# A gated recurrence plus a ternary-weight matmul on eight cores: start-up work reordered, transposed tiles copied out by VectorE

## What is computed

```python
xn = layernorm(x)                                  # x: [8, 4096, 2048] f32
a  = tanh(xn @ Wa.T + ba);  b = tanh(xn @ Wb.T + bb)   # Wa, Wb: [64, 2048]
h_t = a_t * h_(t-1) + b_t                          # scan over the 4096 rows
scale = mean(|weight|)                             # weight: [2048, 2048]
w_t = clip(round(weight / scale), -1, 1)           # -1, 0 or 1
out = x + (xn + h @ Wout.T + bout) + (xn @ (w_t * scale).T + bias)
```

## Time and profile before

| what | value |
| --- | --- |
| median of three runs | 747.67 us |
| the profiled execution | 748.4 us |
| its span on the slowest core (core 6) | 746.9 us |
| spans of the eight cores | 742.0 to 746.9 us |
| mean granted TensorE clock of core 6 | 0.992 |
| PE busy, share of the span | 586.5 us, 79% |
| DVE busy, share of the span | 348.9 us, 47% |
| ACT busy, share of the span | 235.4 us, 32% |

### The profile page before, as it was taken

How to read it: one execution, slowest core, us unless ns; L and a number is a source line. 1 busy time by engine, 2 the same in 40 slices (tenths; PEclk the granted TensorE clock), 3 DMA queues, 4 the chain that set the end, 5 groups by cost and what they waited for, 6 DMA issues and landing times.

```text
span 746.9 us, 11239 instructions; the slowest of 8 cores (742.0 to 746.9 us)
## 1 busy us (share of the span) xinstructions
PE 586.5 (79%) x3740; PEld 310.9 (42%) x3804; DVE 348.9 (47%) x303; ACT 235.4 (32%) x250; POOL 217.9 (29%) x742
## 2 busy tenths in 40 slices
PE   0112202447899999999999999999999999999995
PEld 0111202434444444444454444444444445444442
DVE  0000316985555444555544555544555544555521
ACT  0665302562522323222223332233222222322220
POOL 0000061225043333333333334333333333433400
PEclk9999999999899999999999999999999999999998
DMA  7996008873123343332333333333333233222321
GB/s 234 340 330 196 0 0 278 267 251 106 57 113 117 128 146 141 142 121 114 114 113 113 114 113 114 121 137 139 149 134 113 114 113 114 114 113 113 114 91 79
DMA packets 16831, 103.02 MB, mean 138 GB/s; under 512 B 4326, under 2 KB 4358, under 8 KB 4358
## 3 DMA queue, kind: packets, MB, share of 16 engines
q1 hardware_dynamic: 9350, 51.96, 21.2%
q0 software_dynamic: 7424, 50.34, 17.7%
HBM read 68.73 MB, written 33.55 MB: 137 GB/s over the span
## 4 chain that ended last, share of the span: by engine, by line
PE 65%; DMA 11%; ACT 8%; issue 4%; ACTq 4%; DVEq 3%; DVE 2%; POOLq 2%; SPq 1%; POOL 0%
PE pffn L560 16%; PE pffn L546 15%; PE pffn L556 14%; PE pffn L543 13%; DMA vv<-wf 7%; ACT xnT L302 4%; ACTq L301 3%; PE pab L534 3%; DMA outb<-wf 2%; PE ptr L570 2%; DVE wbn L368 2%; ACT xnT L298 1%; DVEq L367 1%; DMA sqscr<-wf 1%; DVEq L362 1%
## 5 line engine op out<-in xcount | busy, mean ns | idle before, releaser
L560 PE MATMUL pffn<-w_rhs,xnT 128*128 128x512 bf16 x512 | 195.1, 381 | 3.3 <-ACT w_rhs L259 1.7
L546 PE MATMUL pffn<-w_rhs,xnT 128*128 128x512 bf16 x496 | 188.0, 379 | 1.6
L556 PE MATMUL pffn<-w_rhs,xnT 128*128 128x512 bf16 x480 | 182.9, 381 | 0.0
L543 PE MATMUL pffn<-w_rhs,xnT 128*128 128x512 bf16 x465 | 176.2, 379 | 0.0
L346 DVE TENSOR_REDUCE sums<-sx 128x1 f32<-128x2048 f32 x32 | 73.1, 2286 | 140.4 <-DMA sx<-x 140.1
L298 ACT COPY xnT<-ptr 128x1024 bf16<-128x1024 bf16 x31 | 31.4, 1012 | 240.1 <-PE ptr L570 240.1
L605 POOL TENSOR_SCALAR mm_<-sums 128x1 f32<-128x1 f32 x32 | 7.4, 232 | 333.8 <-DVE sqscr L348 310.9
L280 ACT ACTIVATE xnb<-sx,nmr,yr 128x2048 bf16<-128x2048 f32 x31 | 64.9, 2093 | 99.5 <-POOLq L639 99.5
L397 DVE SCALAR_TENSOR_TENSOR outb<-pffn,negs,vv 128x1024 f32<-128x1024 f32 x32 | 41.1, 1284 | 117.7 <-PE pffn L586 102.4
L480 PE MATMUL ptr<-sidn,wbn 128*128 128x128 bf16 x256 | 28.3, 296 | 62.5 <-DVE wbn L368 60.2
L556 PEld LDWEIGHTS pffn<-w_rhs,xnT 128*128 128x128 bf16 x512 | 50.3, 98 | 62.5 <-issue 2.9
(11 more groups left out here) (109 smaller groups left out, 587.4 us busy)
## 6 DMA issues: line engine op xcount, KB each, us to landing
sx<-x SPq DMA_DIRECT2D x32, 1024.0 KB, 5.3
y<-outb POOLq DMA_DIRECT2D x32, 1024.0 KB, 5.7
outb<-wf POOLq DMA_DIRECT2D x11, 1024.0 KB, 6.6
wtile<-wf SPq DMA_DIRECT2D x8, 1024.0 KB, 10.9
vv<-wf SPq DMA_DIRECT2D x8, 1024.0 KB, 10.9
sqscr<-wf POOLq DMA_DIRECT2D x5, 1024.0 KB, 6.4
wasb<-wa SPq DMA_DIRECT2D x1, 512.0 KB
wosb<-wout SPq DMA_DIRECT2D x1, 512.0 KB, 11.3
```

Of the source, the lines that this page charges most:

```text
L543: tensor.matmul(pffn[:, 0:512], lhs, w_rhs[:, 2048 * c:2048 * c + 512], start=st_, stop=False)
L546: tensor.matmul(pffn[:, 512:1024], lhs, w_rhs[:, 2048 * c + 512:2048 * c + 1024], start=st_, stop=False)
L556: tensor.matmul(pffn[:, 1024:1536], lhs, w_rhs[:, 2048 * c + 1024:2048 * c + 1536], start=st_, stop=False)
L560: ins = tensor.matmul(pffn[:, 1536:2048], lhs, w_rhs[:, 2048 * c + 1536:2048 * c + 2048], start=st_, stop=False)
```

## The change

The change has two parts.

In the start-up, SP loads `Wout` in 16 pieces at once after the small inputs, then the two x tiles, then `Wb` (after the first cast), and only then the first-pass weight tiles. ACT and PE do `Wa`, `Wb` and `Wout` before the first pass instead of behind it. POOL issues the loads of the second pass first of all, the first three without any wait, and runs `chain` for x tiles 0 and 1 only after all sixteen and the 16 small transfers to `wocv`. DVE computes the sums of x tiles 0 and 1 after the sixteenth ternary tile. PE and ACT do the first x tile after all of the weight. The second half of the columns of tile 0 now follows its first half directly.

In the loop, the two copies from `ptr` to `xnT` go from ACT to DVE, where they stand between the sums of tile k+2 and the two `pffn` instructions.

```diff
 sync:
+            for j in range(NW):
+                sync.dma_start(out=wosb[:, 64 * j:64 * (j + 1)],
+                               in_=wo_d[128 * j:128 * (j + 1), :]
+                               ).then_inc(s_wol, 16)
             sync.dma_start(out=sx[:, 0:D], in_=x_d[0:TT, :]).then_inc(s_x0, 16)
             sync.dma_start(out=sx[:, D:2 * D],
                            in_=x_d[TT:2 * TT, :]).then_inc(s_x1, 16)
+            sync.wait_ge(s_cast, 1)
+            sync.dma_start(out=wasb[:, :], in_=wb_d[:, :]).then_inc(s_wbl, 16)
             for j in range(NW):
...
-            sync.dma_start(
-                out=wosb[:, :].rearrange("p (j s) -> p j s", j=NW),
-                in_=wo_d[:, :].rearrange("(j p) s -> p j s", p=128)
-            ).then_inc(s_wol, 16)
-            sync.wait_ge(s_cast, 1)
-            sync.dma_start(out=wasb[:, :], in_=wb_d[:, :]).then_inc(s_wbl, 16)
 scalar, in the loop:
-                if k < NT - 1:
-                    j = k + 1
-                    jsl = j % 2
-                    scalar.wait_ge(s_tr, 2 * k + 3)
-                    if k >= 1:
-                        scalar.wait_ge(s_ffn, k)
-                    scalar.drain()
-                    scalar.copy(xnT[:, jsl * D:jsl * D + 1024],
-                                ptr[:, 0:1024]).then_inc(s_xnT, 1)
-                    scalar.wait_ge(s_tr, 2 * k + 4)
-                    scalar.drain()
-                    scalar.copy(xnT[:, jsl * D + 1024:jsl * D + 2048],
-                                ptr[:, 1024:2048]).then_inc(s_xnT, 1)
 vector, in the loop:
                 if k < NT - 2:
                     sums_sqs(k + 2)
+                if k < NT - 1:
+                    j = k + 1
+                    jsl = j % 2
+                    vector.wait_ge(s_tr, 2 * k + 3)
+                    if k >= 1:
+                        vector.wait_ge(s_ffn, k)
+                    vector.drain()
+                    vector.tensor_copy(xnT[:, jsl * D:jsl * D + 1024],
+                                       ptr[:, 0:1024]).then_inc(s_xnT, 1)
+                    vector.wait_ge(s_tr, 2 * k + 4)
+                    vector.drain()
+                    vector.tensor_copy(xnT[:, jsl * D + 1024:jsl * D + 2048],
+                                       ptr[:, 1024:2048]).then_inc(s_xnT, 1)
                 vector.wait_ge(s_mix, 2 * k + 1)
 gpsimd:
+            for j in range(NW):
+                if j >= 3:
+                    g.wait_ge(s_tern, j - 2)
...
             chain(0)
             chain(1)
-            for j in range(NW):
-                if j < 3:
-                    g.wait_ge(s_wabs, 10 + 2 * j)
-                    if j == 2:
-                        g.wait_ge(s_sums, 2)
-                else:
-                    g.wait_ge(s_tern, j - 2)
```

More of the change, by code:

```diff
@@ L240, in _ @@
             for j in range(NW):
-                if j == 11:
-                    scalar.wait_ge(s_stats, 1)
-                    scalar.drain()
[L244 to L251, removed]
-                    scalar.wait_ge(s_tr, 2)
-                    scalar.drain()
-                    scalar.copy(xnT[:, 1024:2048], ptr[:, 1024:2048]
-                                ).then_inc(s_xnT, 1)
                 for grp in range(2):
@@ L420, in _ @@
         def _(tensor):
-            tensor.wait_ge(s_ms, 1)
-            for j in range(NW):
-                tensor.wait_ge(s_wabs, j + 1)
-                for c in range(NCH):
-                    ins = tensor.matmul(
-                        spare[:, 0:1],
-                        xnT[:, (j % 2) * D + 128 * c:(j % 2) * D + 128 * (c + 1)],
-                        onescolb[:, :],
-                        start=(j == 0 and c == 0),
-                        stop=(j == NW - 1 and c == NCH - 1))
-                ins.then_inc(s_pam, 1)
             tensor.wait_ge(s_cast, 1)
@@ L452, in _ @@
             ins.then_inc(s_wotr, 1)
+            tensor.wait_ge(s_cvecv, 1)
+            for j in range(NW):
+                tensor.wait_ge(s_wabs, j + 1)
+                for c in range(NCH):
+                    ins = tensor.matmul(
+                        spare[:, 0:1],
+                        xnT[:, (j % 2) * D + 128 * c:(j % 2) * D + 128 * (c + 1)],
+                        onescolb[:, :],
+                        start=(j == 0 and c == 0),
+                        stop=(j == NW - 1 and c == NCH - 1))
+                ins.then_inc(s_pam, 1)
             tensor.wait_ge(s_acc, 16)
@@ L466, in _ @@
                           start=True, stop=True).then_inc(s_bc, 5)
-            def wtr(j):
+            for j in range(NW):
                 sl = j % 2
@@ L484, in wtr @@
                     ins.then_inc(s_wtr, 1)
-            for j in range(13):
-                wtr(j)
-            tensor.wait_ge(s_wtrc, 26)
+            tensor.wait_ge(s_wtrc, 32)
             tensor.wait_ge(s_xnbs, 1)
@@ L551, in _ @@
                 else:
+                    tensor.wait_ge(s_ev, 2 * k - 1)
+                for c in range(NCH):
+                    st_ = (c == 0)
+                    lhs = xnT[:, xo + 128 * c:xo + 128 * (c + 1)]
+                    tensor.matmul(pffn[:, 0:512],
+                                  lhs, w_rhs[:, 2048 * c:2048 * c + 512],
+                                  start=st_, stop=False)
+                    tensor.matmul(pffn[:, 512:1024],
+                                  lhs, w_rhs[:, 2048 * c + 512:2048 * c + 1024],
+                                  start=st_, stop=False)
+                if k >= 1:
                     tensor.wait_ge(s_ev, 2 * k)
@@ L596, in _ @@
             g.memset(two_i[:, :], 2)
+            for j in range(NW):
+                if j >= 3:
+                    g.wait_ge(s_tern, j - 2)
+                sl = j % 3
+                buf = outb if sl < 2 else sqscr
+                so = (sl % 2) * D if sl < 2 else 0
+                g.dma_start(out=buf[:, so:so + D],
+                            in_=wf_d[128 * j:128 * (j + 1), :]
+                            ).then_inc(s_wlb[sl], 16)
+            g.wait_ge(s_cvecv, 1)
+            for i in range(16):
+                g.dma_start(out=wocv[64:65, 128 * i:128 * (i + 1)],
+                            in_=cneg[i:i + 1, :]).then_inc(s_cvr, 16)
             def chain(j):
```

143 lines of the change are left out of this document (53 added, 90 removed).

## The result

| what | before | after |
| --- | --- | --- |
| median | 748.30 us (10 runs) | 757.76 us (9 runs) |
| ratio after / before | 1 | 1.0126, 95% interval 1.0107 to 1.0144 |
| the profiled execution, its slowest core's span | 748.4, 746.9 | 755.74, 754.2 (core 2) |

The change makes the kernel 1.3% slower, 9.4 us by the ratio. 742.4 was forecast. The range of 735 to 777 holds the time, but the likeliest case had the wrong sign. In some runs of most kernels, one of each here, some cores show a lower granted clock and take 5 to 13% longer; the ratios leave such runs out.

What follows compares the result with a forecast made beforehand. PE was taken to bound the loop, transfers and DVE the start-up. Span 746.9 - 18.3 (start-up) + 13.0 (copies) = 741.6 us, 743.1 with 1.5 outside; the profiled execution being 0.7 above the median, 742.4. Range 735 to 777.

Steps and rivals of the forecast that it cites:

- The copies: Loop: 31 pairs of ACT copies become DVE copies of 0.68 us; a turn grows 0.42 us, 13.0 us in all.
- the two-elements-a-step end of the bracket: Loop: lower bound for one DVE copy, 0.15 + 0.53 = 0.68 us; the upper, one element a step, 1.22.
- rival A: Loop: the DVE copy runs at one element a step, 1.22 us; +28.2 us, 776 us in all; chance 18%.
- 2d - 0.94: Loop: growth of each turn in us, d being the time of one DVE copy; 0.42 us at d 0.68.
- The first pass: Start-up: bound by transfers at 3.19 us per MiB; its last tile, 15, reaches ACT at 77.5, 11.1 us later.
- rival B: Start-up: early loads crowd the queues, Wb lands 8 us later, start-up gain only 10 us, 751 us; chance 8%.
- The credit of 2 us for fuller queues: Start-up, first pass: early transfers fill about 5.6 us of unused DMA time, of which 2 us were credited.
- Sum and thresholds: Start-up: PE's sum follows tile 15 at once, at 80.7; thresholds take 4.3 us, first ternary tile at 85.0.
- The second pass: Start-up: sixteen ternary tiles, 3.96 us each less 0.8 us of waits; sixteenth starts at 143.7, ternary at 147.4.
- The uncovered sums: Start-up end: sums of x tile 0 and POOL's chain, no longer hidden under loads, cost 13.7 us, until 161.1.
- From `nmr` to PE's transposes and on to the loop: Start-up end: after normalizing, PE transposes at 163.7; 12.3 + 6.9 us later, at 182.9, the transposes of tile 1.
- Rival C: Loop: DVE's sums come too late for the copies; 1 us past the slack costs 31 us, some 773; chance 5%.

Runs made afterwards that it cites:

- the copies alone: The kernel before with only the two loop copies from ptr to xnT moved from ACT to DVE: 756.27 us, ratio 1.0137.
- the two edits to the queues: The changed kernel with Wout in one transfer and POOL's first three loads held until absolute values 14 to 16: 744.36 us, ratio 0.9986.

## Why the prediction was right and wrong

**The copies: right.** The forecast took 0.68 us for a copy, from the two-elements-a-step end of the bracket, and gave rival A, 1.22, 18%. Measured was 0.692. The turn grew by 0.33 us where 2d - 0.94 gives 0.44 with the measured d. The 0.1 is the hand-over from L392 to PE, 0.15 us here and 0.25 in the sum. Thirty turns make 10 us, and 10.2 were measured for the copies alone. The 13.0 us of core 2 equal the forecast's 13.0 by coincidence: 3 of them are the late first turns.

On this copy the trace decides between two sentences of one page of the Trainium skill, VectorE: DVE Perf Modes. Its tier table ("The perf-mode tier table (the rule you actually need)"), up to two elements a cycle from PSUM, agrees with 692 ns for 1024 elements; "Rules for kernel authors", "Either accept 1× (PSUM src)", does not hold for this bf16 copy. The estimate of 0.66 us by the page's formula was 0.03 too low.

**The first pass: wrong, and the step that failed.** It is "Wb lands as the last of 6.5 MiB, 20.7 us of transfers that begin some 4 us in, at about 25". `Wb` was there at 32.5. Two things in the step were mis-sized. One is its price, 3.19 us for each MiB, read in the settled first pass of before: from 5 to 35 us the DMA engines were as busy as there and moved 275 GB/s, 3.8 us for each MiB. What slows them is open. The other is that the step took every issue as given and `Wb` as the end of the line. SyncE's 16 small issues took 13.28 us behind POOL's loads, so that `Wb` was issued only at 19.00; then four first-pass tiles were issued right behind it, from 19.52 on, and `Wb` took 13.4 us to land among them. That is rival B, 7.5 us of its 8, and it had 8%. Its "against" ("the bytes ahead of Wb are small beside those 8 us, 2.5 MiB") is what misled: at the forecast's own price 2.5 MiB are 8.0 us, and the step itself had counted 6.5 MiB. The credit of 2 us for fuller queues did not come either; the slices moved less. The rest of the pass was 45.9 us from first to last absolute value where 42.5 were forecast, 3.3 more. A standstill lies in it, for which the forecast charged 0.3 us: from 44 to 46 us nothing is moved (0 GB/s), since all four buffers are full and SyncE issues the next load only at 44.34, when ACT has done the first tile; how the 3.3 us divide was not tried. Together 10.7 us: 88.2 and not 77.5. That the crowding causes it is shown by the two edits to the queues, which brought the first ternary tile from 95.67 to 84.19.

**Sum and thresholds: right.** 95.67 - 88.22 = 7.45 us from the last absolute value to the first ternary tile, 7.5 forecast. **The second pass: right but for a rest.** From the first ternary tile to the last `wbn`'s end 62.6 us, 62.4 forecast.

**The uncovered sums: the mechanism right, the size off by 2.8 us.** 13.7 were taken from the earlier trace rows, 16.5 it was. POOL starts `chain` at 165.79, 2.9 us after DVE's sums have ended, though its last issue was done by 157.41. It is 2.9 us on all eight cores, wherever the last issue ends, and before it was 0.3. Why it starts late stays open. **From `nmr` to PE's transposes and on to the loop** 2.4 and 17.7 us, 2.6 and 19.2 forecast.

The misses of the start-up are 10.7 + 0.2 + 2.8 - 0.2 - 1.5 = 12.0 us, and 12.0 is what 194.91 lies behind the 182.9 forecast.

**Rival C: true at a few turns.** It was priced as a loss at every turn. In the settled loop DVE stands idle for 2.29 us before its first copy, as argued, but at the first turns the load lands late and the two copies leave no room for it. It had 5%.

**The chances.** "At d = 0.77 the change is worth nothing" stated how thin the case was: a difference of 5 us in either term. A start-up gain built of seven steps, one of them a transfer among transfers of other engines, was not known to 4 us, yet its bounds were put at -14 and -22. With bounds that took rival B in, -8 to -22, the likeliest case would have had both signs.

## What to carry to other kernels

A transfer that is issued early was not free here: it delayed the small ones behind it that a chain waited for, and that showed as long issues on SyncE's queue. So issue it when its buffer is needed and look what stands last in that line and what is issued right behind it. Count what an engine does ahead of the instruction that frees the bottleneck's buffer, not how busy it is: two copies there lost 10 us, one, with the other on a second engine, won 10. Work that waits for nothing, such as the sums of the first x tiles, belongs into a stretch that is bound by transfers, and never behind its end.

## What was not expected of the hardware

Two things. The time that SyncE needs to issue a transfer depended on what was queued already, in other queues too: the issue of an x tile takes 0.42 us in before, took 3.20 us right behind `Wout` in one transfer, and 11.48 us there with POOL's 3 MiB outstanding as well. And a pause of PE of 2.00 us in each turn of 20.5 us cost more than itself: the granted clock fell to half, 1.2 GHz, for some 3.4 us as PE went on, and a turn was 3.2 us longer than in the kernel before (20.48 against 17.28). A pause of 0.75 us in each turn of 17.63 left the clock at 1.00.
